# Graph attention with a pre-norm on one core: the first q chunk one unit later, one x tile loaded ahead of the k copies, and scores divided over two units where V is projected

## The chip, the cores and the metric

The kernel runs on one core of a Trainium2 chip. The metric is the time of one execution on the device in microseconds; the lower the better. Three runs of the kernel before took 4095.68 to 4096.75 us, with a median of 4096.61 us.

## What is computed

For each of 16 batches, x is 1024 rows by 512. The rows are normalised, clipped at zero, projected to q, k and v (8 heads of 64), masked attention over 1024 nodes follows, and x is added:

```python
h = jnp.maximum(_layernorm(x, axis=-1), 0.0)
q = (h @ Wq + bq).reshape(b, n, 8, 64)          # k and v alike
scores = jnp.einsum('bihd,bjhd->bhij', q, k) / 8.0
scores = scores + jnp.where(adj == 0, -1e9, 0.0)
out = jnp.einsum('bhij,bjhd->bihd', softmax(scores), v)
x = x + out.reshape(b, n, 512)
```

## The kernel before, in words

Every product is made of rounded operands in two parts: a high part (a rounded copy, on ScalarE) and a low part (what the rounding lost, on VectorE or GpSimd). One float32 product becomes two or three matmuls.

**Units.** A batch is 128 units, four pairs of heads with 32 units each; a unit's place in its pair is called v, its place in the batch u. The five engines each run through the same list of units, in an order written out by hand, and meet at semaphores. In unit u TensorE contracts the probabilities of unit u - 2 with V in two matmuls into the bank O (L571, then L578), and between them turns four 128x128 tiles of probabilities for unit u into one of two halves of T (L559, which waits until unit u - 2's low part is made). ScalarE copies T's half to pT (high part, L679) and VectorE subtracts (low part, L847). In every even unit TensorE also makes a block of scores, four 128x512 matmuls (L547, L548) into one of two halves of S; VectorE adds the mask and takes the row maximum (L841), and one score block later ScalarE takes the exponential (L687).

**Work put in between.** The bank misc is one bank for everything else, and each user waits until the user before it has left (`before`). In pair p the q and k of pair p + 1 are projected, in four chunks of 12 matmuls (L517), each divided over two units, `QK_SLOTS`. The chunks are k first half (k=0), q first half (1), q second half (2), k second half (3). In a chunk's second unit (`QK_AT`) ScalarE moves it from misc to `proj` (L702), one and two units later it copies the two heads' high parts (L713: to qA or kA on partitions 0 to 63, to qB or kB on partitions 64 to 127). VectorE makes q's low parts (L823), GpSimd k's (L400); then the SP queue's DMAs copy k to the other partitions (`copy_k`, L241), and the first score of the next pair, at v = 22, waits for these copies. At v = 2 and 10 the finished output is turned through misc (L587), and ScalarE copies it out (L670) after that unit's L679 and L687. V is projected in 12 matmuls a tile (L530) in units 121, 123 to 127, and 0 and 1 of the batch itself; VectorE adds the bias and frees misc (L834), ScalarE and GpSimd divide it into parts (L728, L387).

**The next batch's x.** In units 5, 7, 11, 13, 37, 39, 43 and 45 VectorE takes the statistics of a tile of x (`stats`, L805 and L808), after that unit's L847 and its `low_q`. From unit 75 on GpSimd normalises a tile (L381) and two units later TensorE turns it (L496, units 77, 79, 83, 85, ...). Two buffers hold these tiles; the SP queue reloads one (L222) when the tile in it has been turned. At unit 79 (v = 15 of pair 2) it issues the copies of k's second half first, which wait for GpSimd's L400, and tile 3's load after them.

The last batch has no next one: its statistics, turns and V projections for a next batch, and the chunks of its last pair, are left out. There are 63 pairs projected inside the batches.

Of the kernel before, what the change touches and what calls it, by code (L numbers as in the profile page):

```python
# [38 lines left out]
PAIRS = H // 2  # L39
# [3 lines left out]
SBLOCKS = H * NB  # L43
# [13 lines left out]
CHUNKS = ((1, 0), (0, 0), (0, 1), (1, 1))  # L57
Q_CHUNKS = [k for k, (w, _) in enumerate(CHUNKS) if w == 0]
K_CHUNKS = [k for k, (w, _) in enumerate(CHUNKS) if w == 1]
QK_SLOTS = ((3, 4), (5, 6), (8, 9), (11, 12))  # L60
QK_START = {32 * p + s: (p, k) for p in range(PAIRS) for k, (s, _) in enumerate(QK_SLOTS)}
QK_AT = {32 * p + s: (p, k) for p in range(PAIRS) for k, (_, s) in enumerate(QK_SLOTS)}

HIGH_AFTER = (1, 2)
LOW_AFTER = (1, 3)

HT_SLOTS = (77, 79, 83, 85, 88, 91, 94, 96)
HT_AT = {s: t for t, s in enumerate(HT_SLOTS)}
# [2 lines left out]
STATS_SLOTS = (5, 7, 11, 13, 37, 39, 43, 45)  # L71
STATS_AT = {s: t for t, s in enumerate(STATS_SLOTS)}

COPY_K_AT, STORE_AT, RES_AT, WQK_AT = (8, 15), 19, 24, (21, 21, 28, 21)

OUT_AT, FINISH_AT = (2, 10), (3, 17)
PER = UNITS // PAIRS
# [4 lines left out]
V_EARLY = len(V_SLOTS)  # L82
V_AT = {s: (1, j) for j, s in enumerate(V_SLOTS)} | {j: (0, V_EARLY + j) for j in range(NB - V_EARLY)}
V_SPLIT_AT = {s + 1: v for s, v in V_AT.items() if s + 1 < UNITS} | {0: (0, V_EARLY - 1)}
XLN = 2
XLN_USES = [len(range(r, NB, XLN)) for r in range(XLN)]


def some(n):

    return not (isinstance(n, int) and n <= 0)


def adj_preln_kernel(nc, x, adj, Wq, bq, Wk, bk, Wv, bv, out):
    with ExitStack() as ctx:
# [75 lines left out]
        q_low, k_low, k_copied = sem("q_low"), sem("k_low"), sem("k_copied")  # L171
        v_mm, v_biased, v_hi, v_ready = sem("v_mm"), sem("v_biased"), sem("v_hi"), sem("v_ready")
        scored, shifted, exped = sem("scored"), sem("shifted"), sem("exped")
# [17 lines left out]
        def x_tile(b, t):  # L191

            return xln[:, t % XLN, :] if some(b) else x0[t // GB][:, t % GB, :]

# [23 lines left out]
        def _(sp):  # L218
            def load_xln(b, t):

                sp.sem_inc(sp_passed)
                sp.dma_start(xln[:, t % XLN, :], x[b, t * P:(t + 1) * P, :]).then_inc(xln_in[t % XLN], 16)  # L222

# [9 lines left out]
            def copy_k(b, p, half):  # L233

                cols = slice(half * HALF, (half + 1) * HALF)

                sp.wait_ge(k_low, 4 * (PAIRS * b + p) + 2 * (half + 1))
                for second in range(2):
                    _, k = qk_buffers(p, second)
                    own, other = (slice(0, HD), slice(HD, P))[::-1 if second else 1]  # L240
                    sp.dma_start(k[other, :, cols].bitcast(F32), k[own, :, cols].bitcast(F32)  # L241
                                 ).then_inc(k_copied, 16)
# [61 lines left out]
            def body(b, first=False, last=False):  # L304
                for u in range(UNITS):
                    p, v = u // 32, u % 32
                    if u == 0 and not first and not last:
                        sp.wait_ge(h_turned, NB * (b + 1))
                        for t in range(XLN):
                            load_xln(b + 1, t)  # L310
                    if u % NB == LAG and not (first and u == LAG):
                        if u == LAG:
                            move_o(b - 1, GROUPS - 1)
                        else:
                            move_o(b, u // NB - 1)
                    if v == STORE_AT and not (first and p == 0):

                        sp.wait_ge(y_added, 2 * (PAIRS * b + p))
                        if p == 0:
                            store(b - 1, PAIRS - 1)  # L320
                        else:
                            store(b, p - 1)
                    if v == RES_AT and not (first and p == 0):
                        sp.wait_ge(stored, 16 * (PAIRS * b + p))
                        load_xres(b, p)
                    if u in STATS_AT and not last:
                        t = STATS_AT[u]
                        sp.wait_ge(bn_done, NB * (b + 1) + t + 1)
                        load_xln(b + 1, (t + XLN) % NB)
                    for half in range(2):  # L330
                        if v == COPY_K_AT[half] and not (last and p == PAIRS - 1):
                            copy_k(b, p + 1, half)
                    if u in HT_AT and HT_AT[u] + XLN < NB and not last:
                        t = HT_AT[u]
                        sp.wait_ge(h_turned, NB * (b + 1) + t + 1)
                        load_xln(b + 1, t + XLN)
                    if v == WQK_AT[p] and not (last and p >= PAIRS - 2):

                        sp.wait_ge(qk_mm, 4 * (PAIRS * b + p + 1) + 4)
                        load_wqk((p + 2) % PAIRS)  # L340
# [13 lines left out]
        def _(gp):  # L354
# [50 lines left out]
            def sum_o(b, g, last=False):  # L405
# [3 lines left out]
                if second:  # L409
# [4 lines left out]
                    elif g // 4 == 3 and not last:  # L414
                        gp.wait_ge(v_ready, NB * (b + 1) + len([s for s in V_SPLIT_AT if NB * g < s < NB * g + NB + LAG + 3]))
                    else:
# [38 lines left out]
            def body(b, first=False, last=False):  # L455
                for u in range(UNITS):
# [7 lines left out]
                    if u in NORM_AT and not last:  # L464
                        normalise(b + 1, NORM_AT[u])
                    if u in V_SPLIT_AT and not (last and u > V_FROM):
                        nxt, j = V_SPLIT_AT[u]
                        split_v(b + nxt, j)
# [20 lines left out]
        def _(pe):  # L489
# [41 lines left out]
                                   start=n == 0, stop=n == len(parts) - 1)  # L531
                mm.then_inc(v_mm, 1)

            def score(b, s):

                n = SBLOCKS * b + s
                q, k = qk_buffers(s // 16, (s // 8) % 2)
                i = s % NB
                pair = PAIRS * b + s // 16
                pe.wait_ge(q_low, 4 * pair + 3 + (s // 8) % 2)  # L540
                pe.wait_ge(k_copied, 64 * (pair + 1))
                if some(n - 1):
                    pe.wait_ge(exped, n - 1)
                for half in range(2):
                    cols = slice(half * HALF, (half + 1) * HALF)
                    dst = S[:, s % 2, cols]
                    pe.matmul(dst, q[:, i * P:(i + 1) * P], k[:, 0, cols], start=True, stop=False)  # L547
                    mm = pe.matmul(dst, q[:, i * P:(i + 1) * P], k[:, 1, cols], start=False, stop=True)  # L548
                mm.then_inc(scored, 1)

            def turn_probs(b, u):

# [36 lines left out]

            def score_ahead(b, u, last):  # L590
                s = u // 2 + LEAD
                if u % 2 == 0 and s < SBLOCKS:
                    score(b, s)
                if u % 2 == 0 and s >= SBLOCKS and not last:
                    score(b + 1, s - SBLOCKS)

            def fill(b, u, last):
                if u in V_AT and not (last and u >= V_FROM):
# [58 lines left out]
        def _(act):  # L657
# [101 lines left out]
            def body(b, first=False, last=False):  # L759
                for u in range(UNITS):  # L760
# [12 lines left out]
                    if u >= PER and u % PER in OUT_AT:  # L773
                        copy_y(b, u // PER - 1, OUT_AT.index(u % PER))
                    if u in V_SPLIT_AT and not (last and u > V_FROM):
                        nxt, j = V_SPLIT_AT[u]
                        v_high(b + nxt, j)
# [20 lines left out]
        def _(dve):  # L798
# [17 lines left out]
            def low_q(b, p, k, second):  # L816

                n, half = 4 * (PAIRS * b + p) + k, CHUNKS[k][1]
                cols = slice(half * HALF, (half + 1) * HALF)
                q, _ = qk_buffers(p, second)  # L820
                at = HD * second
                dve.wait_ge(qk_high, 2 * n + 1 + second)
                dve.tensor_tensor(q[HD - at:2 * HD - at, cols], proj[at:at + HD, k % 2, :],  # L823
                                  q[at:at + HD, cols].bitcast(F32), ALU.subtract).then_inc(q_low, 1)
# [73 lines left out]
            def body(b, first=False, last=False):  # L898
                for u in range(UNITS):
                    if u == LAG + 2 and not first:  # L900
                        invert(b - 1, GROUPS - 1)
                    if u > LAG + 2 and u % NB == LAG + 2:
                        invert(b, u // NB - 1)
                    if u - 1 in HT_AT and not last:
                        h_low(b + 1, HT_AT[u - 1])
                    probs_low(b, u)
                    s = u // 2 + LEAD
                    if u % 2 == 0 and s < SBLOCKS:
                        shift(b, s)
                    if u % 2 == 0 and s >= SBLOCKS and not last:  # L910
                        shift(b + 1, s - SBLOCKS)
                    if u in V_AT and not (last and u >= V_FROM):
                        bias_v(b + V_AT[u][0], V_AT[u][1])
                    for second in range(2):
                        v = u - LOW_AFTER[second]
                        if v in QK_AT and QK_AT[v][1] in Q_CHUNKS and not (last and QK_AT[v][0] == PAIRS - 1):
                            low_q(b, QK_AT[v][0] + 1, QK_AT[v][1], second)
                    if u in STATS_AT and not last:
                        stats(b + 1, STATS_AT[u])

# [25 lines left out]
```

## Time and profile before

| | before |
|---|---|
| median of three runs | 4096.61 us |
| the profiled execution | 4094.8 us, its span 4093.0 us |
| granted TensorE clock, mean | 0.996 of full speed |
| TensorE matmul busy | 4027.1 us, 98% |
| TensorE weight load busy | 3279.4 us, 80% |
| VectorE, ScalarE, GpSimd busy | 3100.4 us (76%), 3075.5 us (75%), 1394.2 us (34%) |

The span is the time from the first to the last instruction; the profiled execution is 1.8 us longer than it. A row of the timeline has the start, the time taken from start to the end of the last of its instructions, the engine, the line, the operation, the tiles and the count; behind it in brackets the idle time of the engine before it and who ended it. Matmuls are pipelined, so a row of TensorE can be longer than the step to the next row. Batch 6 of the 16 runs from 1580.2 us on; its unit 5 begins at about 1596 us, units 9 to 13 lie between 1606 and 1617 us, and unit 85 begins at about 1741 us.

### The profile page before, as it was taken

How to read it: one execution, taken by the hardware profiler on the slowest of the kernel's cores; microseconds unless marked ns; L12 is line 12 of the kernel's file. 1: busy time of each engine (PE TensorE's matmuls, PEld its weight loads, DVE VectorE, ACT ScalarE, POOL GpSimd, SP SyncE). 2: the span in 40 equal slices, each digit the busy share in tenths (PEclk: the TensorE clock that was granted, in tenths of full speed). 3: DMA queues.
4: the chain of work that ended last, by engine and by line, in shares of the span. 5: the costliest groups of instructions: out<-in, count | busy, mean ns of one | idle time of the engine just before them, and what ended most of it. 6: DMA issues, size and time to landing. Idle time of an engine off the chain costs nothing.

```text
span 4093.0 us, 77408 instructions
## 1 busy us (share of the span) xinstructions
PE 4027.1 (98%) x22016; PEld 3279.4 (80%) x22016; DVE 3100.4 (76%) x5128; ACT 3075.5 (75%) x5514; POOL 1394.2 (34%) x1409
## 2 busy tenths in 40 slices
PE   7999999999999999999999999999999999999998
PEld 6888888878887888878888788887888878888886
DVE  6877878777777777768777687776877868778686
ACT  5877868778686786867868688686886868868687
POOL 4333333333333333323333333332333333333322
PEclk9999999999999999999999999999999999999999
DMA  5232322322222222223222232222322323223121
GB/s 181 69 92 63 85 65 77 86 66 83 80 64 84 72 82 81 62 80 84 70 81 70 73 91 62 81 80 63 92 65 77 84 57 92 77 65 92 44 73 47
DMA packets 240106, 316.30 MB, mean 77 GB/s; under 512 B 16400, under 2 KB 147472, under 8 KB 231056
## 3 DMA queue, kind: packets, MB, share of 16 engines
q1 hardware_dynamic: 239632, 310.71, 26.6%
q8 instruction: 209, 3.42, 0.4%
q14 instruction: 265, 2.17, 0.2%
HBM read 172.23 MB, written 37.75 MB: 51 GB/s over the span
## 4 chain that ended last, share of the span: by engine, by line
PE 81%; issue 9%; POOL 5%; DMA 2%; ACT 2%; SPq 1%; DVE 0%; POOLq 0%; ACTq 0%; DVEq 0%
PE T L559 18%; PE misc L517 14%; PE S L547 10%; PE S L548 10%; PE O L571 10%; PE O L578 10%; PE misc L530 8%; DMA xln<-in_x 1%; POOL kB L400 1%; POOL kA L400 1%; PE misc L587 1%; PE misc L496 1%; POOL xln L381 1%; ACT y L670 1%; POOL outs L420 1%
## 5 line engine op out<-in xcount | busy, mean ns | idle before, releaser
L847 DVE TENSOR_TENSOR pT<-T,pT 128x512 fp32r<-128x512 f32 x2048 | 1390.7, 688 | 712.5 <-ACT pT L679 699.7
L679 ACT CAST pT<-T 128x512 fp32r<-128x512 f32 x2048 | 1185.5, 590 | 671.1 <-PE T L559 573.6
L841 DVE CUSTOM_DVE_ANT_0 S<-S,mask 128x1024 f32<-128x1024 f32 x1024 | 1257.2, 1228 | 9.0 <-PE S L548 8.1
L559 PE MATMUL T<-ident,probs 128*128 128x128 f32 x8192 | 1233.9, 273 | 0.6 <-DVE pT L847 0.2
L559 PEld LDWEIGHTS T<-ident,probs 128*128 128x128 f32 x8192 | 1005.1, 140 | 279.7 <-DVE pT L847 36.4
L687 ACT ACTIVATE probs<-S,negmax 128x1024 f32<-128x1024 f32 x1024 | 1151.6, 1125 | 8.3 <-DVE negmax L841 5.1
L578 PE MATMUL O<-pT,vs 128*64 128x512 f32 x2048 | 965.6, 471 | 0.2 <-DVE pT L847 0.2
L571 PE MATMUL O<-pT,vs 128*128 128x512 f32 x2048 | 816.9, 399 | 14.7 <-issue 14.6
L517 PE MATMUL misc<-hT,wqk 128*128 128x512 f32 x3036 | 789.7, 395 | 4.3 <-ACT y L670 0.8
L517 PEld LDWEIGHTS misc<-hT,wqk 128*128 128x128 f32 x3036 | 557.0, 188 | 156.5 <-ACT y L670 18.4
L420 POOL TENSOR_TENSOR outs<-outs,oT 64x512 f32<-64x512 f32 x256 | 331.7, 1296 | 560.8 <-DMA outs<-oT 539.7
L571 PEld LDWEIGHTS O<-pT,vs 128*128 128x128 f32 x2048 | 386.0, 188 | 80.3 <-issue 17.1
L547 PE MATMUL S<-kA,qA 128*128 128x512 f32 x1024 | 417.4, 408 | 5.8 <-ACT probs L687 3.1
L547 PE MATMUL S<-kB,qB 128*128 128x512 f32 x1024 | 414.7, 405 | 0.0
L548 PE MATMUL S<-kA,qA 128*128 128x512 f32 x1024 | 405.6, 396 | 0.0
L548 PE MATMUL S<-kB,qB 128*128 128x512 f32 x1024 | 402.0, 393 | 0.0
L530 PE MATMUL misc<-wv,hT 128*128 128x512 f32 x1476 | 363.4, 395 | 1.5 <-issue 1.5
L400 POOL TENSOR_TENSOR kA<-proj,kA 64x512 fp32r<-64x512 f32 x128 | 165.6, 1294 | 565.6 <-ACT kB L713 565.6
L387 POOL TENSOR_TENSOR vs<-proj,vs 128x512 fp32r<-128x512 f32 x128 | 168.4, 1316 | 498.4 <-ACT vs L728 498.2
L530 PEld LDWEIGHTS misc<-wv,hT 128*128 128x128 f32 x1476 | 275.0, 189 | 74.2 <-issue 15.9
L702 ACT ACTIVATE proj<-misc,bqk 128x512 f32<-128x512 f32 x253 | 174.2, 689 | 171.7 <-PE misc L517 171.7
L430 POOL TENSOR_TENSOR y<-y,rinv 128x512 f32<-128x512 f32 x128 | 133.8, 1045 | 473.5 <-ACT y L670 459.2
(70 smaller groups left out, 3590.3 us busy)
## 6 DMA issues: line engine op xcount, KB each, us to landing
wqk<-wqk_split SPq DMA_DIRECT2D x63, 1024.0 KB, 6.5
xln<-in_x SPq DMA_DIRECT2D x240, 256.0 KB, 2.6
outs<-in_x SPq DMA_DIRECT2D x66, 512.0 KB, 4.5
kA<-kA SPq DMA_DIRECT2D x128, 256.0 KB, 3.2
kB<-kB SPq DMA_DIRECT2D x128, 256.0 KB, 3.9
outs<-oT SPq DMA_DIRECT2D x256, 128.0 KB, 3.4
out<-outs SPq DMA_DIRECT2D x64, 512.0 KB, 4.0
probs<-in_adj SPq DMA_DIRECT2D x4, 1024.0 KB, 5.0
```

The lines of the kernel that those rows point to most:

```text
L420: gp.tensor_tensor(oP[rows, half, :], oP[rows, half, :], oT[rows, :], ALU.add).then_inc(o_summed, 1)
L517: mm = pe.matmul(bank, wqk[:, w, c, wl, :], hT[:, hl, c, cols], start=n == 0, stop=n == len(parts) - 1)
L530: mm = pe.matmul(bank, hT[:, hl, c, j * P:(j + 1) * P], wv[:, wl, c, :], start=n == 0, stop=n == len(parts) - 1)
L547: pe.matmul(dst, q[:, i * P:(i + 1) * P], k[:, 0, cols], start=True, stop=False)
L548: mm = pe.matmul(dst, q[:, i * P:(i + 1) * P], k[:, 1, cols], start=False, stop=True)
L559: mm = pe.transpose(T[:, u % 2, i * P:(i + 1) * P], probs[:, (GB * g + i) % RING, j * P:(j + 1) * P], ident[:])
L571: pe.matmul(O[:], vs[:, j, head, :], pT[:, u % PT, 0, :], start=j == 0, stop=j == NB - 1)
L578: pe.matmul(O[:HD, :], vs[:, j, head, :HD], pT[:, u % PT, 1, :], start=False, stop=j == NB - 1, skip_group_check=j == NB - 1).then_inc(con ...
L679: act.copy(pT[:, u % PT, 0, :], T[:, u % 2, :]).then_inc(p_hi, 1)
L687: act.activation(probs[:, s % RING, :], S[:, s % 2, :], ACT.Exp, bias=negmax[:, s % RING:s % RING + 1], scale=-1.0, accum_out=rowsum[:, s ...
L841: dve.tensor_tensor_reduce(S[:, s % 2, :], S[:, s % 2, :], mask[:, s % NB, :], 1.0, 3.0e38, ALU.add, ALU.min, negmax[:, s % RING:s % RING ...
L847: dve.tensor_tensor(pT[:, u % PT, 1, :], T[:, u % 2, :], pT[:, u % PT, 0, :].bitcast(F32), ALU.subtract).then_inc(p_lo, 1)
```

## The change

It has three parts. The first q chunk moves from units 5 and 6 of a pair to 6 and 7, and with it ScalarE's evacuation (unit 6 to 7) and high copies (7 and 8 to 8 and 9). VectorE's `low_q` moves from units 7 and 9 (chunk 1) and 10 and 12 (chunk 2) to 8 and 10, and 11 and 13. The copies of k's second half move from v = 15 to v = 16, and stand behind the load of x in the code; v = 15 and 16 differ for the SP queue's order at unit 79 alone. In units 122 to 127, and 0 and 1, a block of scores is divided: its first two matmuls in the even unit, the last two in the odd one, and VectorE's L841 follows in the odd unit.

```diff
-QK_SLOTS = ((3, 4), (5, 6), (8, 9), (11, 12))
+QK_SLOTS = ((3, 4), (6, 7), (8, 9), (11, 12))
-LOW_AFTER = (1, 3)
+LOW_AT = {8: (1, 0), 10: (1, 1), 11: (2, 0), 13: (2, 1)}
-COPY_K_AT, STORE_AT, RES_AT, WQK_AT = (8, 15), 19, 24, (21, 21, 28, 21)
+COPY_K_AT, STORE_AT, RES_AT, WQK_AT = (8, 16), 19, 24, (21, 21, 28, 21)
+HALVED = (122, 124, 126, 0)
...
-                    for half in range(2):
-                        if v == COPY_K_AT[half] and not (last and p == PAIRS - 1):
-                            copy_k(b, p + 1, half)
                     if u in HT_AT and HT_AT[u] + XLN < NB and not last:
                         t = HT_AT[u]
                         sp.wait_ge(h_turned, NB * (b + 1) + t + 1)
                         load_xln(b + 1, t + XLN)
+                    for half in range(2):
+                        if v == COPY_K_AT[half] and not (last and p == PAIRS - 1):
+                            copy_k(b, p + 1, half)
...
-            def score(b, s):
+            def score(b, s, halves=(0, 1)):
...
-                pe.wait_ge(q_low, 4 * pair + 3 + (s // 8) % 2)
-                pe.wait_ge(k_copied, 64 * (pair + 1))
-                if some(n - 1):
-                    pe.wait_ge(exped, n - 1)
-                for half in range(2):
+                if 0 in halves:
+                    pe.wait_ge(q_low, 4 * pair + 3 + (s // 8) % 2)
+                    pe.wait_ge(k_copied, 64 * (pair + 1))
+                    if some(n - 1):
+                        pe.wait_ge(exped, n - 1)
+                for half in halves:
...
-                mm.then_inc(scored, 1)
+                if 1 in halves:
+                    mm.then_inc(scored, 1)
...
             def score_ahead(b, u, last):
                 s = u // 2 + LEAD
-                if u % 2 == 0 and s < SBLOCKS:
-                    score(b, s)
+                halves = (u % 2,) if u // 2 * 2 in HALVED else (0, 1) if u % 2 == 0 else ()
+                if halves and s < SBLOCKS:
+                    score(b, s, halves)
...
-                    if u % 2 == 0 and s < SBLOCKS:
+                    due = u % 2 == (1 if u // 2 * 2 in HALVED else 0)
+                    if due and s < SBLOCKS:
                         shift(b, s)
...
-                    for second in range(2):
-                        v = u - LOW_AFTER[second]
-                        if v in QK_AT and QK_AT[v][1] in Q_CHUNKS and not (last and QK_AT[v][0] == PAIRS - 1):
-                            low_q(b, QK_AT[v][0] + 1, QK_AT[v][1], second)
+                    if u % PER in LOW_AT and not (last and u // PER == PAIRS - 1):
+                        low_q(b, u // PER + 1, *LOW_AT[u % PER])
```

## Rows read from the trace of the kernel before

**Rows 1.** The page's first part: busy time and share of each engine.

```profile
PE 4027.1 (98%) x22016; PEld 3279.4 (80%) x22016; DVE 3100.4 (76%) x5128; ACT 3075.5 (75%) x5514; POOL 1394.2 (34%) x1409
```

**Rows 2.** Waits: engine line, who ended it: us in total, times, longest.

```profile
PEld misc L496 <- POOL xln L381: 15.7, 15, 1.5
...
PE misc L496 <- POOL xln L381: 10.3, 15, 1.1
...
PE S L547 <- DMA kB<-kB: 2.5, 4, 1.9
```

**Rows 3.** Timeline of PE, batch 6: first q/k chunk matmuls in units 5, 11, 37.

```profile
1596.71 0.47 PE L578 MATMUL O<-pT,vs 128*64 128x512 f32 x1
1597.22 1.65 PE L517 MATMUL misc<-hT,wqk 128*128 128x512 f32 x6
...
1611.13 0.48 PE L578 MATMUL O<-pT,vs 128*64 128x512 f32 x1
1611.44 1.55 PE L517 MATMUL misc<-hT,wqk 128*128 128x512 f32 x6
...
1653.02 0.48 PE L578 MATMUL O<-pT,vs 128*64 128x512 f32 x1
1653.38 1.66 PE L517 MATMUL misc<-hT,wqk 128*128 128x512 f32 x6
```

**Rows 4.** Timeline of PE, batch 5: V tiles of units 123 and 125.

```profile
1560.39 2.90 PE L530 MATMUL misc<-wv,hT 128*128 128x512 f32 x12
...
1568.29 0.47 PE L578 MATMUL O<-pT,vs 128*64 128x512 f32 x1
1568.74 2.97 PE L530 MATMUL misc<-wv,hT 128*128 128x512 f32 x12
```

**Rows 5.** Timeline of SP and POOL, batch 6: x tile 3 loaded and normalised.

```profile
1737.96 0.46 SPq L222 DMA_DIRECT2D xln<-in_x  x1
...
1742.37 0.77 POOL L381 TENSOR_SCALAR xln<-xln,negmean,rstd 128x512 f32<-128x512 f32 x1 [2.61 <-DMA xln<-in_x]
```

**Rows 6.** Timeline of ACT, units 9 and 10.

```profile
1608.47 0.69 ACT L702 ACTIVATE proj<-misc,bqk 128x512 f32<-128x512 f32 x1 [0.31 <-PE misc L517]
1609.06 0.58 ACT L679 CAST pT<-T 128x512 fp32r<-128x512 f32 x1
...
1610.63 0.59 ACT L670 COPY y<-misc 128x512 f32<-128x512 f32 x1
```

**Rows 7.** Timeline of ACT, units 6 to 8.

```profile
1602.10 0.69 ACT L702 ACTIVATE proj<-misc,bqk 128x512 f32<-128x512 f32 x1 [0.83 <-PE misc L517]
1602.82 0.62 ACT L713 CAST kB<-proj 64x512 fp32r<-64x512 f32 x1
1603.45 0.59 ACT L679 CAST pT<-T 128x512 fp32r<-128x512 f32 x1
1604.07 0.62 ACT L713 CAST qA<-proj 64x512 fp32r<-64x512 f32 x1
1604.59 0.57 ACT L679 CAST pT<-T 128x512 fp32r<-128x512 f32 x1
```

**Rows 8.** Timeline of DVE, from unit 13's low part to unit 14's.

```profile
1617.51 0.69 DVE L847 TENSOR_TENSOR pT<-T,pT 128x512 fp32r<-128x512 f32 x1 [0.27 <-ACT pT L679]
...
1619.05 0.69 DVE L847 TENSOR_TENSOR pT<-T,pT 128x512 fp32r<-128x512 f32 x1
```

**Rows 9.** Timeline of DVE, from unit 7's low part to unit 8's.

```profile
1604.07 0.69 DVE L847 TENSOR_TENSOR pT<-T,pT 128x512 fp32r<-128x512 f32 x1 [1.90 <-ACT pT L679]
...
1606.46 0.69 DVE L847 TENSOR_TENSOR pT<-T,pT 128x512 fp32r<-128x512 f32 x1
```

**Rows 10.** Timeline of PE, the turns of units 16 and 19, and DVE ahead of 19.

```profile
1619.89 0.63 PE L559 MATMUL T<-ident,probs 128*128 128x128 f32 x4
...
1623.73 1.29 DVE L847 TENSOR_TENSOR pT<-T,pT 128x512 fp32r<-128x512 f32 x2 [0.38 <-ACT pT L679]
...
1624.48 0.65 PE L559 MATMUL T<-ident,probs 128*128 128x128 f32 x4
```

More of the change, by code:

```diff
@@ L591, in score_ahead @@
                 s = u // 2 + LEAD
-                if u % 2 == 0 and s < SBLOCKS:
-                    score(b, s)
-                if u % 2 == 0 and s >= SBLOCKS and not last:
-                    score(b + 1, s - SBLOCKS)
+                halves = (u % 2,) if u // 2 * 2 in HALVED else (0, 1) if u % 2 == 0 else ()
+                if halves and s < SBLOCKS:
+                    score(b, s, halves)
+                if halves and s >= SBLOCKS and not last:
+                    score(b + 1, s - SBLOCKS, halves)
             def fill(b, u, last):
@@ L907, in body @@
                     s = u // 2 + LEAD
-                    if u % 2 == 0 and s < SBLOCKS:
+                    due = u % 2 == (1 if u // 2 * 2 in HALVED else 0)
+                    if due and s < SBLOCKS:
                         shift(b, s)
-                    if u % 2 == 0 and s >= SBLOCKS and not last:
+                    if due and s >= SBLOCKS and not last:
                         shift(b + 1, s - SBLOCKS)
```

## The prediction

> **What bounds the kernel now.** I read the page first: TensorE's matmuls are busy 98% of the span, all other engines at most 80% [rows 1]. So time is won where TensorE stands between matmuls, and lost where a new wait stops it; what the other engines do is free as long as it is ready on time. The table of waits comes next [rows 2]. It names one wait that the change goes for (the turn of an x tile, L496, which waits for GpSimd's normalised tile, 15 times, once a batch) and one that stands close to it (the first score of a pair, waiting for the copies of k, 4 times). Short waits hide in that table, since ends of matmuls are modelled; so I read the timeline of one whole batch and compared groups of the same matmuls with one another. The reader should see in [rows 3] that a chunk's six matmuls begin 0.31 us behind L578 and take 1.55 us when nothing is late (unit 11), and that both numbers are larger in units 5 and 37; the same in [rows 4] for V. [Rows 6 to 10] are the queues of ScalarE and VectorE just ahead of two places where TensorE waits for them. The pattern repeats from batch to batch.
>
> **Part 1, what the later chunk gives back.** In unit 5 the first q chunk wants misc while ScalarE still evacuates the chunk of unit 4. It starts 1597.22 - 1596.71 = 0.51 us behind L578 instead of 0.31, and takes 1.65 instead of 1.55: 0.30 us lost [rows 3]. In unit 37 it is 0.36 and 1.66: 0.16 us, and units 69 and 101 are like 37. One unit later a whole block of scores lies between the two users of misc, and both waits go: 16 x 0.30 + 47 x 0.16 = 12.3 us. The chunk behind it begins in unit 8 after scores too, so nothing is late there.
>
> **Part 1, what it costs on ScalarE.** The second high copy of this chunk (L713, to qB) moves from unit 8 to unit 9, behind the evacuation of the next chunk (L702) and ahead of unit 10's L679. Units 9 and 10 are the tightest place of that engine: the evacuation waits for TensorE, and from then on L679, L687 and the output's copy L670 run without a gap [rows 6]. L670 ends at 1610.63 + 0.59 = 1611.22; the chunk of unit 11, which needs misc, starts at 1611.44 [rows 3]. A release takes some 0.06 us: the first of two L847 that take 1.29 together and 0.69 alone ends at 1624.42, and the turn that waits for it begins at 1624.48 [rows 10]. So the slack is 0.16 us. What the added copy takes is shown two units earlier: from L702 over kB's copy to L679 is 1603.45 - 1602.10 = 1.35 us [rows 7], without it 1609.06 - 1608.47 = 0.59 [rows 6]. It adds 0.76 us, and TensorE stands 0.76 - 0.16 = 0.60 us in units 11, 43, 75 and 107. That is 62 times (63 projected pairs, less the first batch's first, which has no output to turn): **37.2 us**. From below: the copy to the other partitions steps only 1604.59 - 1604.07 = 0.52 us [rows 7], which leaves 0.36 us, or 22.3 us in all. From above: no slack, 0.76 us, 47.1 us. I take 0.60, because kB's copy behind L702 is the same sequence on the same partitions as qB's will be.
>
> The Trainium skill (ScalarE: Activation LUTs, "What ACT_TABLE_LOAD costs") gives an ACTIVATE with immediate operands 186 ns + 0.833 ns per element, less some 93 ns when back to back. For 512 elements that is an estimate of 0.52 us, and by it this term would be 22.3 us; the trace has 0.52 for qA's copy and 1.35 - 0.59 = 0.76 for kB's, so the page's figure holds for one of the two sorts only.
>
> **Part 1, what it costs on VectorE.** The low part of chunk 2 for qB leaves unit 12 and stands in unit 13, between that unit's L847 and, in units 13 and 45, the statistics. Unit 13's L847 can't start sooner, as it waits 0.27 us for ScalarE, whose L679 is queued behind an evacuation [rows 8]. So what stood in unit 12 for nothing now pushes unit 14's L847. From L847 over statistics alone to L847 takes 1619.05 - 1617.51 = 1.54 us [rows 8]; with a `low_q` between, 1606.46 - 1604.07 = 2.39 [rows 9]. That is 0.85 later. Unit 14's low part ends at 1619.74 and unit 16's turn, which waits for it, begins at 1619.89 [rows 10]: with a release of 0.06 the slack is 0.09. TensorE stands 0.76 us in units 16 and 48 of 15 batches: **22.8 us**. From below: a step of 0.61 us (0.69 less the 0.08 by which two L847 overlap, 2 x 0.69 - 1.29 [rows 10]), less 0.09, is 15.6 us; from above, 0.85 without slack, 25.5 us. In units 77 and 109 no statistics follow, and one `low_q` takes their place: nothing. The other moved `low_q` (units 8, 10 and 11) fall where a half chunk of 1.55 us keeps TensorE longer [rows 3], and VectorE is back in step by unit 13: nothing. If that cover went, the cost would be like that of unit 13.
> GpSimd's L400 of the last chunk is queued behind the statistics' follow-up, so the copies of k come up to 0.85 us later too; TensorE arrives 0.76 later itself. The four waits of [rows 2] grow by 0.1 each; I leave that out.
>
> **Part 2, x tile 3.** Its load stands behind k's copies, which wait for GpSimd, and starts at 1737.96, though the tile that it replaces was turned in unit 79, more than a unit before these copies can start. GpSimd stood idle 2.61 us until it landed [rows 5], so nothing else of GpSimd's was in the way. Issued 1.2 us sooner (the 15.7 us over 15 waits are 1.05 each) it would be ready in time; the turn of unit 79 comes before GpSimd's two L400, so I expect more than that, and the wait of L496 goes: between 10.3 us (matmuls) and 15.7 us (weight loads) [rows 2], and I take the middle, **13.0 us**, as either engine's own wait counts only part. The lower bound is 0 if GpSimd's order holds it. What is passed: SP issues one DMA (0.46 us of its queue) ahead of k's copies, which still wait for GpSimd then; and their scores come only at unit 86, six units on. Nothing is late next. At the other units v = 15 or 16 changes no order.
>
> **Part 3, divided scores.** In unit 123 twelve V matmuls take 2.90 us. In unit 125 they start 0.45 behind L578, 0.14 more than the 0.31 of [rows 3], and take 2.97 [rows 4]: 0.21 us lost waiting for the bias of the tile before. The same holds in units 127 and 1. Two score matmuls (half of the four) put 0.45 us between, by the step of such matmuls, (2.90 - 1.55) / 6 = 0.225 us [rows 3, 4], and the tile would start at 1568.29 + 0.31 + 0.45 = 1569.05, behind the 1568.74 at which misc was free. In the even units two remain, again 0.45 more than an odd unit had: free too. 30 x 0.21 + 16 x 0.21 = **9.7 us**. VectorE's L841 stands ahead of the bias now, but it can run beside V's 2.90 us of matmuls, which have to end before the bias anyway. Without that cover the bias would be late by the length of L841 in each tile. No matmul, weight load or semaphore is added, so the lower bound is 0 won.
>
> **The sum.** Won 12.3 + 13.0 + 9.7 = 35.0 us. Lost 37.2 + 22.8 = 60.0 us. Net 25.0 us: the profiled execution goes from 4094.8 (span 4093.0) to 4119.8. The median of the runs is 1.8 us above that execution, so 4121.6 us.
>
> **The rivals.**
> *A, ScalarE's copy is the cheap sort*, 0.52 us. For it: qA's copy. Against it: kB's. 22.3 + 22.8 - 35.0 = +10.1: 4106.7 us. The page named above would have this.
> *B, ScalarE's copy is hidden* and the kernel ends **faster**: place, unit 9; the copy would have to run in the 0.31 us in which ScalarE waits for TensorE, or the output's copy not be what unit 11 waits for. 22.8 - 35.0 = -12.2: 4084.4 us. It decides once the added time at L670 is under 0.16 + 12.2 / 62 = 0.36 us. Against it: the copy is queued behind the evacuation that ends this idle time.
> *C, VectorE's addition is hidden*, say because the statistics or L847 start sooner: 37.2 - 35.0 = +2.2: 4098.8 us. Against: 0.09 us of slack.
> *D, both are hidden* and only the gains stand: 4061.6 us. For it: every one of them is under a microsecond and worked out from one batch.
> *E, x tile 3 stays late* through GpSimd's order or contention among DMAs: 25.0 + 13.0 = +38.0: 4134.6 us. Against: 2.61 us of idle GpSimd.
> *F, the change doesn't free misc*: the chunk in unit 6 still waits. Then 12.3 us less are won: 4133.9 us. Against: unit 11 starts on time with less between.
>
> **How the numbers follow.** Chances: forecast 0.57, A 0.11, B 0.07, C 0.08, D 0.07, E 0.06, F 0.04. A measurement of this kernel can tell about 0.2%, 8.2 us, from no change. The forecast's own range is 4108 to 4133: with VectorE's term at 15.6 and the V term won a bit higher it is some 9 lower, with no slack in ScalarE's (47.1) 10 higher. The whole range runs from 4098 (C) to 4136 (E); B, D and tails are left out. Slower: forecast, E, F and most of A, less tails, 0.71. Within 0.2%: C, some of A, and tails, 0.15. Faster: B and D, 0.14.
>
> **What would show it.** In the changed kernel's timeline: unit 11's chunk starts 0.9 instead of 0.31 us behind L578, with L713 to qB between L702 and L679 on ScalarE. The turn of unit 16 begins 0.06 us behind unit 14's L847, 0.76 late, in the batches' first two pairs alone. The waits of L496 for L381 are gone, L222's load of tile 3 is issued before k's copies, V's groups take 2.90 us all, and the waits of L517 for L670 and of L559 for L847 have grown. I am wrong if unit 11's chunk still starts 0.31 behind L578, or if the turn of unit 16 doesn't move.

## The result, and the profile after

The changed kernel takes 4126.73 us (median of four runs, 4125.22 to 4127.82) where the kernel before took 4096.68 beside it: ratio 1.0075, 95% interval 1.0061 to 1.0089. It is slower, by 30 us. Its profiled execution took 4125.22 us with a span of 4123.4; that of before 4094.8 and 4093.0.

The page of the changed kernel, its first part:

```profile
PE 4014.6 (97%) x22016; PEld 3280.4 (80%) x22016; DVE 3070.6 (74%) x5128; ACT 3084.1 (75%) x5514; POOL 1359.3 (33%) x1409
```

The same instructions are issued, and TensorE is busy for 12.5 us less while the span is 30.4 us longer [rows 1]. So TensorE stands still for some 43 us more. Lines have moved: L562 is now the turn of probabilities (L559 before), L518 the q and k chunks (L517), L531 V (L530), L574 and L581 the contraction (L571, L578), L497 the turn of x (L496); on ScalarE L683 the high part (L679), L691 the exponential (L687), L706 the evacuation (L702), L717 the high copy (L713), L674 the output's copy (L670); on VectorE L851 the low part (L847), L827 `low_q` (L823), L845 the row maximum (L841).

The table of waits of the changed kernel, TensorE's matmuls (us in total, times, longest; "issue" is a wait for nothing that the profile shows):

```profile
PE misc L518 <- ACT y L674: 41.7, 67, 0.7
PE T L562 <- DVE pT L851: 21.1, 31, 0.9
...
PE O L574 <- issue: 3.9, 6, 0.9
```

The two new waits are the two that were forecast: before, L517 waited 0.8 us for L670 and L559 0.2 us for L847. The wait of the x tile [rows 2] is gone from the table. The third line is one that I had not spoken of: it stood at 14.6 us before.

Where it lies in the units shows once the two timelines are cut at the first L559 (L562) of each unit and the units of all 16 batches are added:

| units | change in TensorE's time, all batches | forecast |
|---|---|---|
| 5 and 7, and their likes at 37, 69, 101 | 87.3 - 98.9 = -11.6 us | -12.3 |
| 11, 43, 75, 107 | +55.2 us (13.3, 14.2, 14.1 and 13.5) | +37.2 |
| 15 and 47 (the turns of 16 and 48 come late) | +25.4 us | +22.8 |
| 85 | -13.5 us | -13.0 |
| 122 to 127, 0 and 1 | -22.6 us | -9.7 |
| sum | +32.9 us | +25.0 |

Of the difference to 30.4 us, 0.9 us lies ahead of the first unit, and 1.9 in units 22 and 54, where the first score of a pair no longer waits for k's copies [rows 2]; the rest is spread over other units.

Unit 11 in batch 6 of the changed kernel, ScalarE:

```profile
1620.60 0.69 ACT L706 ACTIVATE proj<-misc,bqk 128x512 f32<-128x512 f32 x1 [0.31 <-PE misc L518]
1621.31 0.62 ACT L717 CAST qB<-proj 64x512 fp32r<-64x512 f32 x1
1621.95 0.59 ACT L683 CAST pT<-T 128x512 fp32r<-128x512 f32 x1
1622.56 1.11 ACT L691 ACTIVATE probs<-S,negmax 128x1024 f32<-128x1024 f32 x1
...
1623.67 0.57 ACT L674 COPY y<-misc 128x512 f32<-128x512 f32 x1
```

and TensorE:

```profile
1623.25 0.48 PE L581 MATMUL O<-pT,vs 128*64 128x512 f32 x1
1624.39 0.47 PE L518 MATMUL misc<-hT,wqk 128*128 128x512 f32 x1 [0.66 <-ACT y L674]
```

The copy to qB stands between the evacuation and L683, as read from the diff. From L706 to L674 it is now 3.07 us where it was 2.16 [rows 6], and the chunk starts 1.14 us behind L581 instead of 0.31 [rows 3].

Units 13 to 16, VectorE and then TensorE:

```profile
1630.51 0.69 DVE L851 TENSOR_TENSOR pT<-T,pT 128x512 fp32r<-128x512 f32 x1 [0.73 <-ACT pT L683]
1631.23 0.69 DVE L827 TENSOR_TENSOR qB<-proj,qB 64x512 fp32r<-64x512 f32 x1
1631.95 0.69 DVE L809 BATCH_NORM_STATS2 bn<-xln 128x6 f32<-128x512 f32 x1
...
1632.89 0.69 DVE L851 TENSOR_TENSOR pT<-T,pT 128x512 fp32r<-128x512 f32 x1
```

```profile
1632.64 0.40 PE L574 MATMUL O<-pT,vs 128*128 128x512 f32 x1
1633.73 0.63 PE L562 MATMUL T<-ident,probs 128*128 128x128 f32 x4 [0.69 <-DVE pT L851]
```

From L851 to L851 it is 2.38 us, as in [rows 9] and not as in [rows 8]; the first ends at 1632.89 + 0.69 = 1633.58 and the turn begins 0.15 later.

### The profile page after: what moved, and what is told of

It reads as the page before. It is cut to its first block, busy times and chain, and to the rows that moved or that the text cites. A ratio compares the mean times of both kernels' runs of the same rounds, so it can differ in the third digit from the quotient of the medians.

```text
span 4123.4 us, 77408 instructions
## 1 busy us (share of the span) xinstructions
PE 4014.6 (97%) x22016; PEld 3280.4 (80%) x22016; DVE 3070.6 (74%) x5128; ACT 3084.1 (75%) x5514; POOL 1359.3 (33%) x1409
## 4 chain that ended last, share of the span: by engine, by line
PE 90%; issue 3%; ACT 3%; DVE 2%; POOL 1%; DMA 0%; ACTq 0%; DVEq 0%; POOLq 0%; SPq 0%
PE T L562 20%; PE misc L518 17%; PE S L549 11%; PE S L550 11%; PE O L581 10%; PE O L574 10%; PE misc L531 8%; PE misc L497 1%; ACT y L674 1%; PE misc L590 1%; ACT probs L691 1%; ACT pT L683 1%; DVE pT L851 1%; DVE bn L809 1%; DVE qB L827 1%
## 5 line engine op out<-in xcount | busy, mean ns | idle before, releaser
L851 DVE TENSOR_TENSOR pT<-T,pT 128x512 fp32r<-128x512 f32 x2048 | 1391.3, 688 | 830.4 <-ACT pT L683 809.3
L683 ACT CAST pT<-T 128x512 fp32r<-128x512 f32 x2048 | 1189.4, 591 | 630.6 <-PE T L562 541.3
L845 DVE CUSTOM_DVE_ANT_0 S<-S,mask 128x1024 f32<-128x1024 f32 x1024 | 1256.8, 1227 | 3.6 <-PE S L550 3.1
L562 PE MATMUL T<-ident,probs 128*128 128x128 f32 x8192 | 1233.1, 273 | 21.4 <-DVE pT L851 21.1
L562 PEld LDWEIGHTS T<-ident,probs 128*128 128x128 f32 x8192 | 1004.8, 140 | 305.6 <-DVE pT L851 36.4
L691 ACT ACTIVATE probs<-S,negmax 128x1024 f32<-128x1024 f32 x1024 | 1150.6, 1124 | 9.3 <-DVE negmax L845 4.5
L581 PE MATMUL O<-pT,vs 128*64 128x512 f32 x2048 | 964.8, 471 | 0.2 <-DVE pT L851 0.2
L518 PE MATMUL misc<-hT,wqk 128*128 128x512 f32 x3036 | 787.6, 395 | 44.7 <-ACT y L674 41.7
L574 PE MATMUL O<-pT,vs 128*128 128x512 f32 x2048 | 816.6, 399 | 3.9 <-issue 3.9
L518 PEld LDWEIGHTS misc<-hT,wqk 128*128 128x128 f32 x3036 | 561.8, 188 | 196.2 <-issue 64.3
L421 POOL TENSOR_TENSOR outs<-outs,oT 64x512 f32<-64x512 f32 x256 | 329.1, 1286 | 620.8 <-DMA outs<-oT 599.7
L574 PEld LDWEIGHTS O<-pT,vs 128*128 128x128 f32 x2048 | 386.0, 188 | 69.9 <-issue 6.4
L531 PE MATMUL misc<-wv,hT 128*128 128x512 f32 x1476 | 359.8, 392 | 4.7 <-issue 4.7
L531 PEld LDWEIGHTS misc<-wv,hT 128*128 128x128 f32 x1476 | 277.4, 188 | 67.9 <-issue 7.6
L706 ACT ACTIVATE proj<-misc,bqk 128x512 f32<-128x512 f32 x253 | 174.2, 688 | 184.3 <-PE misc L518 184.3
```

Of the source, the lines that this page charges most:

```text
L421: gp.tensor_tensor(oP[rows, half, :], oP[rows, half, :], oT[rows, :], ALU.add).then_inc(o_summed, 1)
L518: mm = pe.matmul(bank, wqk[:, w, c, wl, :], hT[:, hl, c, cols], start=n == 0, stop=n == len(parts) - 1)
L531: mm = pe.matmul(bank, hT[:, hl, c, j * P:(j + 1) * P], wv[:, wl, c, :], start=n == 0, stop=n == len(parts) - 1)
L562: mm = pe.transpose(T[:, u % 2, i * P:(i + 1) * P], probs[:, (GB * g + i) % RING, j * P:(j + 1) * P], ident[:])
L574: pe.matmul(O[:], vs[:, j, head, :], pT[:, u % PT, 0, :], start=j == 0, stop=j == NB - 1)
L581: pe.matmul(O[:HD, :], vs[:, j, head, :HD], pT[:, u % PT, 1, :], start=False, stop=j == NB - 1, skip_group_check=j == NB - 1).then_inc(con ...
```

## The experiments

Each starts from the changed kernel unless it says otherwise. Each was timed beside the kernel before; the ratio is to that.

**Part 1 alone.** The chunk, its copies and low parts as changed; no divided scores; the x tile's load behind k's copies.

```diff
-HALVED = (122, 124, 126, 0)
+HALVED = ()
-COPY_K_AT, STORE_AT, RES_AT, WQK_AT = (8, 16), 19, 24, (21, 21, 28, 21)
+COPY_K_AT, STORE_AT, RES_AT, WQK_AT = (8, 15), 19, 24, (21, 21, 28, 21)
...
                     for half in range(2):
                         if v == COPY_K_AT[half] and not (last and p == PAIRS - 1):
                             copy_k(b, p + 1, half)
                     if u in HT_AT and HT_AT[u] + XLN < NB and not last:
```

> Part 1 alone (the q chunk in units 6 and 7, its copies and low parts as in the changed kernel). Theory: each part's cost and gain is its own, so this shows the chunk's gain (11.6 us by the two timelines, units 5 to 7) and both queue costs (55.2 us in units 11, 43, 75, 107 and 25.4 us in units 15 and 47): +69 us on 4096.7, 4166 us. Rival: part of the loss in the changed kernel comes of the other parts (divided scores, k's copies later); then this stands well under 4155.

Measured: 4151.03 us, ratio 1.0139 (1.0122 to 1.0156), some 56 us slower. By units, the three terms come out as in the changed kernel to 0.4 us: -11.6 in units 5, 7 and their likes, +54.8 in units 11, 43, 75 and 107, +25.3 in units 15 and 47. Neither theory had the number: the expectation left out 9.4 us that this run wins at the ends of the loop (units 127 and 0), which I had put down to the divided scores. The time lies 4 us under the rival's 4155, but the rival's reason was not the one: nothing of the loss belongs to the other parts.

**Part 2 alone.** The kernel before with the load ahead of k's copies and these at v = 16.

```diff
-QK_SLOTS = ((3, 4), (6, 7), (8, 9), (11, 12))
-LOW_AT = {8: (1, 0), 10: (1, 1), 11: (2, 0), 13: (2, 1)}
+QK_SLOTS = ((3, 4), (5, 6), (8, 9), (11, 12))
+LOW_AT = {7: (1, 0), 9: (1, 1), 10: (2, 0), 12: (2, 1)}
-HALVED = (122, 124, 126, 0)
+HALVED = ()
```

> Part 2 alone (x tile 3 loaded ahead of k's copies). Theory: the wait of unit 85 goes and nothing else moves: -13 us, 4083.5 us. Rival: k's copies come later for it and the first score of a pair waits more: over 4090.

Measured: 4082.31 us, ratio 0.9969 (0.9958 to 0.9980). As the theory said: unit 85 is 13.5 us shorter over all batches, no other unit changes by more than 1.2.

**Part 3 alone.** As the run before, with the order of SP as before the change, and the scores divided.

```diff
-HALVED = ()
+HALVED = (122, 124, 126, 0)
-COPY_K_AT, STORE_AT, RES_AT, WQK_AT = (8, 16), 19, 24, (21, 21, 28, 21)
+COPY_K_AT, STORE_AT, RES_AT, WQK_AT = (8, 15), 19, 24, (21, 21, 28, 21)
```

> Part 3 alone (scores divided in units 122 to 127, 0 and 1). Theory: the waits for misc go (9.7 us) and so does part of what the end of the loop costs TensorE, since in the changed kernel units 127 and 0 at the seven loop ends are shorter by some 13 us: -22.6 us, 4074 us. Rival: the loop ends' gain came of other parts or of where the instructions lie; then -9.7 us, 4087 us.

Measured: 4081.96 us, ratio 0.9967 (0.9956 to 0.9979), 13 us. Units 122 to 127, 0 and 1 give 12.2 us together, and unit 127 is no shorter at the loop's ends. So the rival was nearer: the 13 us that the changed kernel shows at the loop's ends don't come of this part, or only some 2.3 of them.

**Scores divided in units 122 to 125 alone.** The run before, with two entries fewer.

```diff
-HALVED = (122, 124, 126, 0)
+HALVED = (122, 124)
```

> Scores divided in units 122 to 125 alone, none of the other parts. Theory: only unit 125's wait goes, 15 x 0.21 = 3.2 us, and the loop ends stay as they were: 4093.5 us. Rival: any shift of matmuls ahead of the loop's end shortens it: 4080 us or so.

Measured: 4091.53 us, ratio 0.9991 (0.9981 to 1.0001). Within its interval that is the theory's 3 us and not the rival's 16; by units it is 3.6 us in 122 to 125.

**ScalarE's copy in unit 8.** Both high copies of the moved chunk stand one unit after it.

```diff
                     for second in range(2):
-                        v = u - HIGH_AFTER[second]
-                        if v in QK_AT and not (last and QK_AT[v][0] == PAIRS - 1):
-                            high(b, QK_AT[v][0] + 1, QK_AT[v][1], second)
+                        for v in (u - 1, u - 2):
+                            if v in QK_AT and not (last and QK_AT[v][0] == PAIRS - 1) and (
+                                    u - v == (1 if QK_AT[v][1] == 1 else HIGH_AFTER[second])):
+                                high(b, QK_AT[v][0] + 1, QK_AT[v][1], second)
```

> The changed kernel, with ScalarE's second high copy of the moved chunk in unit 8 (behind the first) instead of unit 9. Theory: the copy was the whole of TensorE's 0.89 us in units 11, 43, 75 and 107, and has room in unit 8; the 0.85 us in units 15 and 47 stay: 4126.7 - 55 = 4071.5 us. Rival: another queue holds the output's copy (VectorE's low parts, misc); then 4105 us or more.

Measured: 4071.47 us, ratio 0.9935 (0.9918 to 0.9951). One moved instruction is worth 55 us, and units 11, 43, 75 and 107 give 54.8 of them. This settles the first cost.

**VectorE's last low part in unit 12 again.**

```diff
-LOW_AT = {8: (1, 0), 10: (1, 1), 11: (2, 0), 13: (2, 1)}
+LOW_AT = {8: (1, 0), 10: (1, 1), 11: (2, 0), 12: (2, 1)}
```

> The changed kernel, with VectorE's last low part of q in unit 12 again instead of 13. Theory: VectorE waits for ScalarE ahead of unit 13's L851 and has room for it there, so the 0.85 us in units 15 and 47 go and nothing else: 4126.7 - 25 = 4101.5 us. Rival: VectorE is full from unit 10 on and the same delay comes out elsewhere: over 4115 us.

Measured: 4114.63 us, ratio 1.0042 (1.0028 to 1.0056): 12 us won, not 25, between the theory and the rival and nearer the rival. Its timeline of VectorE, units 12 and 13, and the sum of GpSimd beside it:

```profile
1627.58 1.08 DVE L827 TENSOR_TENSOR qB<-proj,qB 64x512 fp32r<-64x512 f32 x1
1628.69 0.69 DVE L851 TENSOR_TENSOR pT<-T,pT 128x512 fp32r<-128x512 f32 x1
```

```profile
1626.84 1.27 POOL L421 TENSOR_TENSOR outs<-outs,oT 64x512 f32<-64x512 f32 x1
```

and ScalarE's high part that L851 needs:

```profile
1627.69 0.59 ACT L683 CAST pT<-T 128x512 fp32r<-128x512 f32 x1
```

L851 could have begun at 1628.28 and begins 0.41 us later. VectorE came to unit 12 without a wait since unit 10, and there `low_q` takes 1.08 us instead of 0.69, as it meets GpSimd's L421, which runs until 1628.11. The statistics behind it push unit 14 as before, by half as much. The theory's "has room for it there" was wrong by this.

The Trainium skill (SBUF — State Buffer, "SBUF: two separate sides") says that a VectorE operation with two SBUF inputs and a GpSimd operation that reads SBUF lock a shared pair of ports against one another, and the later one is blocked. By that rule the 1.08 would be 0.53 + 0.69 = 1.22; the trace has 0.14 less, with GpSimd's spans being rough.

**VectorE's low parts in units 8, 9, 10 and 12**, ScalarE as in the change.

```diff
-LOW_AT = {8: (1, 0), 10: (1, 1), 11: (2, 0), 13: (2, 1)}
+LOW_AT = {8: (1, 0), 9: (1, 1), 10: (2, 0), 12: (2, 1)}
```

> The changed kernel with VectorE's low parts in units 8, 9, 10 and 12, and ScalarE's copies left as the change has them. In the run with the last low part in 12 alone half of unit 15's loss stayed: the low part took 1.08 us instead of 0.69 beside GpSimd's sum, and VectorE had come to it without a gap from unit 10 on. Theory: the low part of unit 10 belongs in unit 9, where VectorE waits over 1 us for ScalarE; then it is back in step before unit 12 and units 15 and 47 lose nothing: 4126.7 - 25 = 4101.5 us. Rival: the slow low part in unit 12 alone makes unit 13 late: 4114 us, as there.

Measured: 4101.84 us, ratio 1.0017 (1.0007 to 1.0027). Units 15 and 47 give 24.6 us. This settles the second cost: it was the places of the three low parts alone. The last of them still meets GpSimd's sum in unit 12, where it takes 0.92 us in batch 6, but L851 behind it waits another 0.26 us for ScalarE, so nothing is late: the rival falls.

**The two heads of the moved chunk in the other order.** The copy to qB in unit 8, that to qA in unit 9; what is computed stays.

```diff
-                            high(b, QK_AT[v][0] + 1, QK_AT[v][1], second)
+                            high(b, QK_AT[v][0] + 1, QK_AT[v][1], 1 - second if QK_AT[v][1] == 1 else second)
...
-                if not second:
+                if not second or k == 1:
                     act.wait_ge(qk_evac, 4 * (PAIRS * b + p) + k + 1)
...
-LOW_AT = {8: (1, 0), 10: (1, 1), 11: (2, 0), 13: (2, 1)}
+LOW_AT = {8: (1, 1), 10: (1, 0), 11: (2, 0), 13: (2, 1)}
...
-                dve.wait_ge(qk_high, 2 * n + 1 + second)
+                dve.wait_ge(qk_high, 2 * n + 1 + (1 - second if swapped else second))
```

> The changed kernel with the moved chunk's two heads taken in the other order: the copy to qB (partitions 64 to 127) in unit 8 and the one to qA (0 to 63) in unit 9; the low parts follow. Theory: a copy to partitions 64 to 127 takes the overlap from its own start and from the next two instructions, 0.13 us each, and one to partitions 0 to 63 does not: the cost in unit 9 falls from 0.91 to 0.52 us, TensorE's wait in unit 11 from 0.89 to some 0.45: 4126.7 - 27 = 4099.5 us. Rival: any 64-partition copy behind an evacuation costs this; then 4126 us.

Measured: 4101.53 us, ratio 1.0011 (1.0001 to 1.0020), 2 us from the theory and 25 from the rival. Its ScalarE in units 9 and 10:

```profile
1612.66 0.69 ACT L706 ACTIVATE proj<-misc,bqk 128x512 f32<-128x512 f32 x1 [0.31 <-PE misc L518]
1613.24 0.61 ACT L717 CAST qA<-proj 64x512 fp32r<-64x512 f32 x1
1613.76 0.58 ACT L683 CAST pT<-T 128x512 fp32r<-128x512 f32 x1
1614.23 1.12 ACT L691 ACTIVATE probs<-S,negmax 128x1024 f32<-128x1024 f32 x1
...
1615.34 0.57 ACT L674 COPY y<-misc 128x512 f32<-128x512 f32 x1
```

From L706 to L674 it is 2.68 us: 0.52 more than before the change, where the copy to qB costs 0.91. The three steps are 0.58, 0.52 and 0.47 us, against 0.71, 0.64 and 0.61 in the changed kernel. The copy's length is the same (0.61 and 0.62); what differs is that each next instruction starts before the last one has ended, or only behind it. Unit 11's wait fell to 0.51 us.

**Both queues mended.** The copy in unit 8 and the low parts in 8, 9, 10 and 12.

```diff
-LOW_AT = {8: (1, 0), 10: (1, 1), 11: (2, 0), 13: (2, 1)}
+LOW_AT = {8: (1, 0), 9: (1, 1), 10: (2, 0), 12: (2, 1)}
...
-                        v = u - HIGH_AFTER[second]
-                        if v in QK_AT and not (last and QK_AT[v][0] == PAIRS - 1):
-                            high(b, QK_AT[v][0] + 1, QK_AT[v][1], second)
+                        for v in (u - 1, u - 2):
+                            if v in QK_AT and not (last and QK_AT[v][0] == PAIRS - 1) and (
+                                    u - v == (1 if QK_AT[v][1] == 1 else HIGH_AFTER[second])):
+                                high(b, QK_AT[v][0] + 1, QK_AT[v][1], second)
```

> The changed kernel with both queues mended: the high copy in unit 8, VectorE's low parts in units 8, 9, 10 and 12. Theory: all three parts' gains stand and both costs go: 4126.7 - 55.2 - 25.4 = 4046 us, 1.2% under the kernel before. Rival: one of the waits comes back in another unit: over 4060 us. On the loop's end: if its gain (some 8 us at the seven ends of the loop in the run of part 1 alone) comes of TensorE's order, unit 127 at these ends stays near 5.1 us; if it comes of the stalls themselves, it is back at 6.5.

Measured: 4046.79 us, ratio 0.9874 (0.9858 to 0.9891). This beats both kernels; all of the change's order on TensorE is kept. The waits of its matmuls:

```profile
PE S L497 <- POOL probs L382: 13.9, 2, 12.7
PE O L574 <- issue: 5.1, 6, 1.0
PE misc L590 <- POOL outs L421: 4.6, 1, 4.6
```

Neither of the two new waits is left. The first and the third line are the start of the kernel and its end. On ScalarE L683 starts 0.59 us behind the evacuation again, as in [rows 6] (1592.93 - 1592.34), and L674 2.16 us behind it.

## Why the prediction was right

The direction and the two mechanisms came out, and the time lay in the range; the point was 5 us low (4121.6 against 4126.7). That it came so near is luck: the two costs together are 80.6 us and not 60.0, and a gain of 12.6 us at the ends of the loop, which the forecast did not have, hid more than half of that. Without it the time would have been some 4139 us, above the forecast's own range.

*The two users of misc that no longer meet.* 12.3 us forecast, 11.6 measured, and the same 11.6 in the run of part 1 alone. Rival F falls.

*ScalarE's copy.* The mechanism was right: the run with this one copy moved gives back 55 us. Its size was short: 0.60 us each forecast, 0.89 measured (55.2 / 62). The step of the sum that was mis-sized is "it adds 0.76 us". I added up the steps over the copy and over the L683 behind it, and took the way from there to the output's copy as in [rows 6]. But the third step, L683 to the exponential, is 0.61 instead of 0.47 too, so that 0.91 is added. [Rows 7] held it: behind kB's copy and L679 the next step is 0.62 us, and I read it as belonging to the copy that follows. The slack was mis-sized too: the copy ends at 1624.24 and the chunk begins at 1624.39, 0.15 later and not 0.06, and so in all 62 of these waits (0.14 to 0.15). That leaves 0.08 us of slack instead of 0.16, and a start that is 0.91 - 0.08 = 0.83 late (1.14 - 0.31). The last 0.06 lies in the late chunk itself, where on average the second matmul follows the first by 0.31 us instead of 0.24; I had read this in unit 5, where the six take 1.65 instead of 1.55 [rows 3], and left it out here. Rival A's 0.52 exists, and the run with the heads swapped has it, but for the other head. B and D fall.

*VectorE's low part.* 0.76 us forecast, 25.4 / 30 = 0.85 measured. The push of 0.85 was right (2.38 against 1.54). What was wrong was the slack of 0.09: I took the release of 0.06 us from the turn of unit 19 and used it for the turn of unit 16. There it is 0.15, in all 30 late turns of the changed kernel, and that is just the distance that this turn kept before (1619.89 - 1619.74, [rows 8, 10]). So there was no slack, and what I had called the upper bound, 25.5 us, is what came. C falls by the run with the low parts in 8, 9, 10 and 12. That unit 12 had been free for the low part was true of the order before alone: with the two low parts before it in units 10 and 11 instead of 9 and 10 it isn't, as the run with one low part moved back shows.

*The x tile.* 13.0 us forecast, 13.5 in the changed kernel and in the run of part 2 alone. Rival E falls. The four waits for k's copies, which I had growing, didn't grow: those inside the batches are gone, and the one that is left, of 1.7 us, lies ahead of the first batch.

*The divided scores.* 9.7 us forecast. The run of part 3 alone has 12.2, of which 2.3 lie at the ends of the loop, so 9.9; V's units are 4.10 and 4.09 us long now, odd and even alike.

*What the forecast did not have* is the end of the loop. Batches 1 to 14 are seven turns of a loop of two, so the engines go back to its start six times. In the kernel before, unit 127 at these six ends and the unit 0 behind each take 24.6 us more in all than the same two units elsewhere (unit 127 takes 6.6 us there instead of 3.9). It is 23.9 us with part 2 alone and 22.3 with part 3 alone, but 16.4 with part 1 alone, 12.0 in the changed kernel and 12.4 in the mended one, where unit 127 takes 5.2 us at these ends. The wait of L571 (L574) for nothing that the profile shows is a part of it: 14.6 us over the six ends in the kernel before, 15.2, 13.5, 7.2, 3.9 and 5.1 in the others in the same order. So most of the gain comes with the moved chunk, and not with the stalls of units 11 and 15, which the mended kernel hasn't. It is 24.6 - 12.0 = 12.6 us in the changed kernel. In all these runs the chunk's evacuation on ScalarE and its low parts on VectorE have moved with it, so that not even TensorE's order is singled out as the reason. Why the place of the chunk in units 5 to 7 matters at the end of unit 127 is open; no run here tells.

## What to carry to other kernels

An operation that is moved by one unit on the engine that bounds the kernel takes its followers on other engines with it, and each lands in another queue at another place: look at what stands right behind it there, and who waits for that. Here 12 us won on TensorE cost 80 us on two engines that are busy three quarters of the time, and moving one copy and three low parts back on their queues gave the 80 us back and kept the 12. For the cost of an added instruction, take the way between its neighbours up to the one that is waited for, from a place in the trace where the same sequence stands, and not the first step or two. Take the release, too, from the very wait that is to move and not from another one: 0.06 us against 0.15 was the whole slack here.

## What the hardware showed beyond that

ScalarE: a copy on partitions 64 to 127 starts 0.71 us behind a 0.69 us evacuation, the L683 behind it 0.64 us later, and the exponential 0.61 us after that; with a copy on partitions 0 to 63 these are 0.58, 0.52 and 0.47. So one such copy takes the overlap from three steps, 0.39 us in all, by the two timelines shown above.
The Trainium skill (VectorE: DVE Perf Modes, "Two Vector instructions with no wait between them") says of VectorE that an instruction is held until all before it have finished when one of its inputs (a scalar for each partition counts as one) starts in another quadrant of 32 partitions than the first input that was last read from the same memory, or its output in another one than the last output into the same memory. Read as a rule for ScalarE too, it would hold just these three: the copy itself, L683 by its output, and the exponential by its bias, which comes from partition 0 on. The steps agree. For the third the kernel before has a test in its own trace: in 48 places two L679, which read T alone, stand between kB's copy and the exponential.

```profile
1619.60 0.62 ACT L713 CAST kB<-proj 64x512 fp32r<-64x512 f32 x1
1620.25 1.08 ACT L679 CAST pT<-T 128x512 fp32r<-128x512 f32 x2
1621.35 1.12 ACT L687 ACTIVATE probs<-S,negmax 128x1024 f32<-128x1024 f32 x1
```

The first L679 starts 0.65 us behind the copy, the second 0.49 behind the first (1.08 - 0.59), and the exponential again 0.61 behind the second (1621.35 - 1620.25 - 0.49). So the overlap is back for the second L679 and gone once more for the first instruction that reads a bias after the copy. No run here took the bias away.

VectorE: a `low_q` of 0.69 us took 1.08 us or more where it met a sum on GpSimd that was already under way, in all 30 such places of the run with one low part moved back. In the run with the low parts in units 8, 9, 10 and 12, 33 of them began before the sum that they met, and stayed at 0.69.

A release took about 0.06 us in some places and 0.15 in others. In the changed kernel it is 0.15 us from the end of the low part to the turn in all 30 late turns of units 16 and 48, and 0.14 from the end of the output's copy to the late chunk in all 62, against 0.06 in the turn of unit 19 [rows 10]. How long TensorE stands does not decide it: in the run with one low part moved back, a turn of unit 48 that stood 0.19 us was released in 0.15, and one of unit 15 that stood 0.75 us in 0.06. What the code has to say is that the turns of units 16 and 48 wait for two semaphores (L558, L560) and the others for one; no run here took a wait away to test this, so it stays open.
